# A fused graph-attention and feed-forward block in float32 on one core: the opening of the program is rewritten

## The reference, cut to what matters

```python
x = x + gnn(layernorm(x), adj, adj, Wq, Wk, Wv, bv, Wo, bo)   # x: (128, 128, 384), adj: (128, 128, 128)
x = x + ffn(layernorm(x), Wqk, bqk, Wv, bv, conv_w, conv_b, glob, pos_bias, Wg1, bg1, Wg2, bg2, Wp, bp)

def gnn(x, s, e, ...):                       # 12 heads of 32
    q, k, v = x @ Wq.T, x @ Wk.T, x @ Wv.T + bv
    scores = einsum(q, k) * 384 ** -0.5 + (s + e)
    scores = where(any(scores != 0, -1), scores, -inf)
    return (softmax(scores) @ v) @ Wo.T + bo

def ffn(x, ...):                             # 3 experts of 128, causal attention in each
    gate = softmax(relu(x @ Wg1 + bg1) @ Wg2 + bg2)      # the two largest are kept, softmax over them
    q, k = split(x @ Wqk + bqk)                          # expert 0: a 3-tap convolution over q
    y = [softmax(causal(q_e @ k_e.T * 128 ** -0.5)) @ (x @ Wv[e] + bv[e]) for e in 0, 1, 2]
    return concat(y * w_e) @ Wp + bp
```

## Time and profile before

| | before |
|---|---|
| median of three runs | 2316.46 us (2316.0 to 2317.59) |
| profiled execution, its own time | 2320.13 us |
| its span in the profile | 2318.3 us |
| PE busy | 97% |
| DVE busy | 81% |
| ACT busy | 65% |
| POOL busy | 47% |

### The profile page before, as it was taken

How to read it: one execution, slowest core, us unless ns; L and a number is a source line. 1 busy time by engine, 2 the same in 40 slices (tenths; PEclk the granted TensorE clock), 3 DMA queues, 4 the chain that set the end, 5 groups by cost and what they waited for, 6 DMA issues and landing times.

```text
span 2318.3 us, 51437 instructions
## 1 busy us (share of the span) xinstructions
PE 2238.4 (97%) x16896; PEld 1604.4 (69%) x16896; DVE 1888.0 (81%) x7395; ACT 1504.4 (65%) x5290; POOL 1101.1 (47%) x1353
## 2 busy tenths in 40 slices
PE   2799999999999999999999999999999999999998
PEld 1567777767777667777667777667777667777666
DVE  4788888888888888888888888888888888888884
ACT  2676666776666776666776666766666766666763
POOL 0454544544544544544544545544545444545442
PEclk9899999999999999999999999999999999999999
DMA  5211222211222211222211222212222112222200
GB/s 149 65 48 43 74 74 74 50 53 46 74 74 74 50 45 54 74 74 74 50 47 52 74 74 74 50 42 57 74 74 74 47 46 57 74 74 72 49 15 28
DMA packets 142265, 143.20 MB, mean 62 GB/s; under 512 B 16816, under 2 KB 141360, under 8 KB 142000
## 3 DMA queue, kind: packets, MB, share of 16 engines
q1 hardware_dynamic: 142000, 139.91, 22.7%
HBM read 39.18 MB, written 25.17 MB: 28 GB/s over the span
## 4 chain that ended last, share of the span: by engine, by line
PE 79%; DVE 16%; issue 3%; SPq 1%; ACT 0%; DMA 0%; POOL 0%; DVEq 0%; POOLq 0%
PE A_bank L468 30%; PE B_bank L468 24%; PE A_bank L528 7%; DVE raw_score L832 5%; PE B_bank L547 4%; PE A_bank L540 3%; PE A_bank L515 3%; PE B_bank L522 3%; DVE smax L839 3%; DVE V L821 3%; PE B_bank L532 2%; PE B_bank L494 2%; SPq L439 1%; DVE g_tmp L778 1%; PE A_bank L494 1%
## 5 line engine op out<-in xcount | busy, mean ns | idle before, releaser
L967 POOL TENSOR_TENSOR S<-S,rowf 128x512 f32<-128x512 f32 x384 | 389.4, 1043 | 693.5 <-DVE rowf L858 693.5
L624 ACT ACTIVATE S<-raw_score,smin 128x128 f32<-128x128 f32 x1536 | 593.2, 390 | 141.2 <-DVE smin L832 141.2
L832 DVE CUSTOM_DVE_ANT_0 raw_score<-A_bank,adj,s_unit 128x128 f32<-128x128 f32 x1536 | 444.7, 345 | 32.7 <-PE A_bank L515 32.1
L624 ACT ACTIVATION_READ_ACCUMULATOR S<-raw_score,smin 128x1 f32 x1536 | 292.3, 190 | 0.0
L638 ACT ACTIVATE PT<-A_bank 128x512 f32<-128x512 f32 x384 | 217.2, 592 | 76.9 <-PE A_bank L528 76.9
L839 DVE TENSOR_REDUCE smax<-raw_score 128x4 f32<-128x512 f32 x384 | 258.0, 679 | 0.0
L972 POOL TENSOR_TENSOR S<-S,row2f 128x384 f32<-128x384 f32 x128 | 106.0, 828 | 302.4 <-DVE row2f L866 300.6
L528 PE MATMUL A_bank<-ident,S 128*128 128x128 f32 x1536 | 217.4, 275 | 8.0 <-DVE V L821 5.3
L528 PEld LDWEIGHTS A_bank<-ident,S 128*128 128x128 f32 x1536 | 182.8, 142 | 28.5 <-DVE V L821 5.5
L642 ACT ACTIVATE yT_hi<-B_bank 128x384 fp32r<-128x384 f32 x128 | 62.3, 487 | 173.7 <-PE B_bank L547 173.6
L631 ACT ACTIVATE S<-S,s2min 128x128 f32<-128x128 f32 x384 | 149.0, 391 | 18.8 <-DVE s2min L843 18.6
(11 more groups left out here) (165 smaller groups left out, 6384.6 us busy)
## 6 DMA issues: line engine op xcount, KB each, us to landing
xin<-in_x SPq DMA_DIRECT2D x32, 768.0 KB, 4.7
Qs<-q_hi SPq DMA_DIRECT2D x256, 96.0 KB, 2.2
Ks<-k_hi SPq DMA_DIRECT2D x256, 96.0 KB, 2.7
out<-x1res SPq DMA_DIRECT2D x128, 192.0 KB, 1.9
Qs<-q_lo SPq DMA_DIRECT2D x128, 96.0 KB, 2.2
Ks<-k_lo SPq DMA_DIRECT2D x128, 96.0 KB, 2.2
adj<-in_adj SPq DMA_DIRECT2D x32, 256.0 KB, 3.5
S<-in_wq SPq DMA_DIRECT2D x1, 576.0 KB, 5.9
```

The source lines that it names most:

```text
L624: ins = nc.scalar.activation(S[b % 2][:, h, :], raw_score[c][:, j, :], ACT.Exp, bias=smin[b % 2][:, h:h + 1], scale=-1.0, accum_out=ssum[b ...
L832: ins = nc.vector.tensor_tensor_reduce(raw_score[c][:, j, :], src[:, j * T:(j + 1) * T], adj2[:, b, :], s_unit[:], 3.0e38, ALU.add, ALU.mi ...
L967: nc.gpsimd.tensor_tensor(S[b % 2][:, hs, :], S[b % 2][:, hs, :], rowf[b % 2][:, hs].unsqueeze(2).broadcast_to([P, HPC, T]), ALU.mult).the ...
```

## The change

The opening and the first two turns are rewritten; from turn 2 on the tables of order are as before.

- The maxima cross the partitions over PE: PE transposes the columns of maxima into a PSUM bank (`W.turn`), DVE reduces them to one number each (`top_col`), PE spreads these over all partitions by a matmul with the identity (`W.spread`), and DVE reads the scales from that bank. POOL's `partition_all_reduce` is gone.
- The two sets of weights are now q and k of A (`W.scale.0`) and the other four (`W.scale.1`). A semaphore `wscale_ready` lets ACT begin as soon as the scale is there, and the remaining small operations (`W.unit`) come later.
- Ten loads go to ACT's queue (five small vectors, adj, three weights in four pieces); SP issues the rest. Half of the 12 copies into `Ks` of group 0 are issued from ACT (`W.stack.1`).
- `FIRST_STEPS` gives an order of its own to turns 0 and 1. Splitting of weights (`W.hi`, `W.lo`) is spread between the other steps, `A.hT@1` and `A.qk.0@1` come ahead of the scores of group 0, and the last `qk@1` after them.
- On SP, `adj` of group 1 comes ahead of the 24 copies for group 1. Banks and counts of semaphores follow from the written order over all turns.

```diff
+FIRST_STEPS = {
+    "pe": """
+        W.turn.0@0 W.spread.0@0
+        A.hT.0@0 A.hT.1@0 A.hT.2@0 A.qk.0@0 A.qk.1@0 A.qk.2@0 A.qk.3@0 W.turn.1@0 A.qk.4@0 W.spread.1@0
...
+    "sp": """
+        A.res@0 A.stack.0@0 A.stack.1@0 A.adj@0 A.stack.0@1 A.stack.1@1
+    """,
+}
...
+def whole_program(engine):
+
+    first = [parse(word) for word in FIRST_STEPS.get(engine, "").split()]
+    order = [parse(word) for word in ORDER_OF_STEPS[engine].split()]
+    program = list(first)
+    for turn in range(2 if first else 0, NG + 2):
+        for step in order:
+            group = turn - (0 if ahead(step) else 1 if step[0] == "A" else 2)
+            if 0 <= group < NG:
+                program.append((step, group))
+    return program
...
             sp.dma_start(xin[:], dram_group(x, 0)).then_inc(x_loaded, 16)
-            sp.dma_start(adj2[:], dram_group(adj, 0)).then_inc(adj_loaded, 16)
...
-                        for j in range(HPC):
+                        for j in range(HPC // 2 if g == 0 and b == 1 else HPC):
                             sp.dma_start(heads[n * HD:(n + 1) * HD, :, j, :],
...
+                if stage == "W":
+                    n = scale_part[b].stop - scale_part[b].start
+                    if kind == "turn":
+                        pe.wait_ge(maxima, (2, 6)[b])
+                        nc.tensor.transpose(bank["B"][0][0:n, 0:P], wmax[:, scale_part[b]],
+                                            ident[:]).then_inc(maxima_turned, 1)
+                    else:
+                        pe.wait_ge(tops, b + 1)
+                        nc.tensor.matmul(bank["B"][1][:, 0:n], top_col[0:n, b:b + 1].broadcast_to([n, P]),
+                                         ident[0:n, 0:n], start=True, stop=True).then_inc(tops_spread, 1)
+                    return
...
+            act.dma_start(bqk_col[:], bqk).then_inc(consts_loaded, 16)
...
+            act.dma_start(adj2[:], dram_group(adj, 0)).then_inc(adj_loaded, 16)
+            for n in (4, 5):
+                act.dma_start(staged(raw[n][2], C), raw[n][0]).then_inc(raw_loaded[n], 16)
+            act.dma_start(staged(V2, VG)[:, :, 0:C], wv2).then_inc(raw_loaded[7], 16)
+            act.dma_start(staged(V2, VG)[:, :, C:VG], wg1).then_inc(raw_loaded[7], 16)
...
+            def weight_scales(part):
+                cols = scale_part[part]
+                n = cols.stop - cols.start
+                dve.wait_ge(maxima_turned, part + 1)
+                nc.vector.tensor_reduce(top_col[0:n, part:part + 1], bank["B"][0][0:n, 0:P], AXX,
+                                        ALU.max).then_inc(tops, 1)
+                dve.wait_ge(tops_spread, part + 1)
+                link_scale(nc.vector.tensor_scalar(wtop[:, cols], bank["B"][1][:, 0:n], TINY, None, ALU.max))
...
-            def largest(n):
-
-                pool.wait_ge(maxima, n + 1)
-                nc.gpsimd.partition_all_reduce(wtop[:, 3 * n:3 * n + 3], wmax[:, 3 * n:3 * n + 3], P,
-                                               bass.bass_isa.ReduceOp.max).then_inc(tops, 1)
```

More of the change, by code:

```diff
@@ L124, with parse, ahead @@
 }
[L128 to L136, removed]
+def parse(word):
+    word, _, group = word.partition("@")
+    stage, kind, *at = word.split(".")
+    step = (stage, kind, *([int(n) for n in at] + [0, 0])[:2])
+    return (step, int(group)) if group else step
+def ahead(step):
+    return step[0] == "A" and step[1] in ("hT", "qk", "stack")
+def whole_program(engine):
[8 more added lines that the diff above has]
+    return program
 GATE_LINKS = 17
@@ L286, in build @@
         gate_step, gate_exp = sem("gate_step"), sem("gate_exp")
[L289 to L294, removed]
+        program = {e: whole_program(e) for e in ORDER_OF_STEPS}
         def counted(step):
             return "ahead" if ahead(step) else step[0]
-        jobs = {s: [x for x in ORDER["pe"] if counted(x) == s] for s in products}
@@ L300, in build, with ordinals @@
[L300 to L306, removed]
+        def ordinals(engine, kept):
+            place, n = {}, dict.fromkeys(products, 0)
+            for step, g in program[engine]:
+                if kept(step):
+                    n[counted(step)] += 1
+                    place[step, g] = n[counted(step)]
+            return place
@@ L353, in both @@
-            def both(a, b, last):
-                for step in order:
-                    if ahead(step):
-                        if not last:
-                            do(step, following(a), False)
-                    elif step[0] == "A":
-                        do(step, a, last)
-                    elif b is not None:
-                        do(step, b, last)
-            for step in order:
-                if ahead(step):
-                    do(step, 0, False)
-            both(0, None, False)
@@ L367, in groups @@
-            both(1, 0, False)
-            for a in range(2, NG - 1):
-                both(a, a - 1, False)
-            both(NG - 1, NG - 2, True)
-            for step in order:
-                if step[0] == "B":
-                    do(step, NG - 1, True)
+            for step, g in program[name]:
+                do(step, g, g == NG - 1)
         def dram_group(t, g):
-            if isinstance(g, int):
-                return t[g * GB:(g + 1) * GB].rearrange("b t c -> t b c")
-            i, off = g
```

245 lines of the change are left out of this document (132 added, 113 removed).

## The result

The changed kernel takes 2308.49 us (median of five, 2307.82 to 2309.91). The kernel before, run beside it on the same chip, takes 2317.59 us (2316.0 to 2320.72). The ratio is 0.9957, 95% interval 0.9946 to 0.9969: 9.1 us faster, where 18.5 were forecast (2316.46 less 2298), and outside the range of 2290 to 2306. Its profiled execution took 2309.91 us, with a span of 2308.1.

What follows compares the result with a forecast made beforehand. PE was taken to bound the kernel from turn 2 on, so only turn 2's start moves: 18.1 gained, 2.3 given back, lead 16.1 at DVE's scores, 18.7 at turn 2 (117.39 to 98.7). Median 2316.46 becomes 2298, range 2290 to 2306.

Steps and rivals of the forecast that it cites:

- the waits around the all-reduce: Opening: without POOL's two "issue" waits, 11.63 and 7.56 us, PE's first product starts at 17.1 instead of 35.20, gaining 18.1.
- DVE's scores of group 0: Turn 1: 25.6 us of DVE steps plus 6.4 waiting for ACT's high parts, so the last score ends at 79.7.
- ACT then starts its first split at 13.65: Opening: maxima end at 11.6, DVE's h at 12.45, scales take 1.2; ACT splits at 13.65 instead of 25.91.
- the rival with 4.6 us: Opening: ACT's own ten load issues end at 18.24, delaying everything 4.6, to 2302.4; chance 0.22 together with PE's clock.
- PE's wait for `W.spread.1`: Before k of group 0 is complete: PE waits for DVE's maxima, v's split for second scales; 2.3 us given back.
- the copies were hidden as forecast: K's copies of group 0 land at 39.9, or 43.8 undivided, before PE reaches the scores at 44.9; splitting earns nothing.
- By the same working PE ends proj.3 at about 97: End of turn 1: the rest of group 0 (splits, norm.3, turn, mix, proj) runs beside the copies, ending about 97.
- the copies end last, by 2 us: Group 1's copies with adj take 19.0 us after DVE's last score, so they start turn 2 at 98.7.
- The rival on the clock: PE at half rate between 48 and 80 costs 6 us on group 1's products and proj: 2304; chance 0.22 with ACT's hold.
- The signs of being wrong: Rest after turn 2 changes, PE waits over 2 us between 17 and 39, or turn 2 doesn't wait for the last copy.
- From there the remaining span should be the same, to within 1 us: From PE's first score of group 1 to the end: 2318.3 less 117.4, 2200.9 us, as before.
- The rival with the banks of B: From turn 2 on: shifted loads and bank assignment cost 0.8 us or more per turn, making the kernel slower; chance 0.03.

Runs made afterwards that it cites:

- experiment 1: Changed kernel with ACT's last load, the fourth piece of weights (wg1), moved to the end of SP's list; 2305.6 us, ratio 0.9948.
- experiment 5: Changed kernel with all 24 copies of group 0 issued from SP again, K's undivided; 2308.76 us, ratio 0.9956.
- experiment 10: Experiment 1's kernel with norm.3 before ln2.0, lo.7 before proj.3, 48 unread PE transposes, and adj behind q's twelve copies; 2301.14 us, ratio 0.993.
- experiment 2: Kernel before with only the all-reduce replaced by maxima crossing over PE; order, loads and copies as before; 2306.66 us, ratio 0.9955.
- experiments 9 and 12: Both on experiment 1's kernel. 9: norm.3 first, lo.7 earlier, 48 unread PE transposes, 2305.72 us. 12: only adj behind q's copies, 2306.05 us.
- experiment 11: Changed kernel with all loads back on SP in the order of before, the 12 copies on ACT kept; 2307.12 us, ratio 0.9952.
- experiment 8: Experiment 1's kernel with 48 unread transposes behind turn.2 and mix.2 of group 0 to keep PE busy; 2305.7 us, ratio 0.9943.

## Why the prediction was wrong, step by step

The direction and the mechanism of the first gain, the waits around the all-reduce, were right. The size was wrong by half, and in the trace the loss can be added up. Forecast were 18.7 us at PE's first score of group 1; the spans differ by 10.2 (2318.3 less 2308.1).

| step of the prediction | forecast | measured | lost |
|---|---|---|---|
| first product of PE | 17.1 | 19.88 | 2.8 |
| from there until k is complete | 16.7 | 17.4 | 0.7 |
| from there until DVE's first score | 13.9 | 13.9 | 0 |
| DVE's scores of group 0 | 32.0 | 33.2 | 1.2 |
| from the last one until turn 2 | 19.0 | 18.8 | -0.2 |
| DVE behind PE in turn 2 (lead at B.hT 12.87, not 14.14) | 0 | 1.3 | 1.3 |
| the rest as long as before | 2200.9 | 2204.9, of it 1.3 in the row above | 2.7 |

**"ACT then starts its first split at 13.65" failed.** The scales were better than I took them: x wasn't late (1.1 in the sum), and they stand at 12.47, 1.2 sooner. But ACT was held until 16.42, 3.95 after them. This was the rival with 4.6 us, which shared a chance of 0.22 with PE's clock. It was decided by experiment 1. The Trainium skill, "Perfetto Trace Analysis", section "Per-instruction lifecycle", has the two issuing engines share the block that generates descriptors (its heading names DVE and SP, a note below it SP and ACT, as here). By that rule ACT's last issue was to end about where SP's did, at 18.24; it ended at 16.31, so the trace agrees roughly with the size. But the shared block as the prediction used it, the two queues in turn, isn't the reason: SP's last load is issued by 6.67, and the 8.91 us begin at 7.40. In experiment 1 two queues are busy just the same, and no load's issue takes longer than 1.65 us. What does hold the issue stays open.

**PE's wait for `W.spread.1` was near the forecast, and the copies were hidden as forecast.** k took 17.4 where 16.7 were given. From there K's last copy landed after 8.4 us, not 6.1 (45.7 less 37.3), which cost nothing. `h` of group 1 ended at 44.56, DVE's first score came 13.9 after k, and an undivided set of copies was hidden (experiment 5). The scores took 33.2 instead of 32.0, with ACT's exponentials and DVE in turns in the chain. I haven't taken these two small sizes apart.

**"By the same working PE ends proj.3 at about 97", and "the copies end last, by 2 us", failed.** I had 17.3 us from the last score to the end of `proj.3`; it took 19.0, and in the first profile of before 15.2. PE idles 4.3 us after `turn.2` and then 2.5 more, behind splits of weights that the new order has put on ACT and DVE there. It then works at the lower clock, which costs 1.4 us in `proj.2` (3.22 less 1.82) and 1.3 in `turn.3` (2.76 in the timeline, 1.47 in experiment 10). No run moved the splits. The rival on the clock had put 6 us on the products of group 1. There the clock was low as well,

```profile
61.00:75.00 14.00, 10.05 (x72) 6.80 (x73) 10.45 (x51) 10.05 (x43) 4.22 (x5) 0.76 0.00 1
```

but the chain in that stretch is made of DVE's scores and ACT's exponentials, and PE has time in hand. The price falls where PE is waited for. The copies took 18.4 us from the last score to the last landing (84.41 to 102.8) where I had 19.0, and so it is `proj.3` that ends last, by 0.6. The interval until turn 2, 18.8 for 19.0, was right by luck: it was the length of another chain than the one I had added up.

**What DVE still had to do was left out.** With `proj.3` ending so late, x, `ln2.3` and `lo.7` stand on DVE between it and the first score of group 1: 2.7 us, from 103.45 to 106.14. PE then waits for DVE twice in turn 2, and 1.3 us of the lead are gone at B.hT.

**The signs of being wrong.** The prediction named three, and all three are there. The rest of the span changed (next paragraph). PE idled about 2.3 us between its first product and the end of k (busy for 15.13 of 17.50 us from 19.80 on), beside the 2.8 us by which it began late. And the last copy wasn't what turn 2 waited for.

**"From there the remaining span should be the same, to within 1 us" failed, and this was an error of base.** One profile was taken for the kernel. In a second one the way to turn 2 is 2.7 us shorter (1.1 of it in the two "issue" gaps, 11.34 and 6.74 against 11.63 and 7.56) and the rest 4.0 longer. Against that one the changed kernel's lead at turn 2 is 11.4, not 14.1, and the span's is 11.5. The forecast subtracted a landmark worked out from durations (98.7) from one (117.39) that holds 2.7 us which the second profile doesn't have. For the way to turn 2 it isn't known which of the two is the usual one; for the rest it is the second. The rival with the banks of B, which was to add to each turn, is refuted: from the fourth on, loads of x are on average 69.73 us apart in the first profile of before, 69.79 in the second, and 69.76 and 69.75 in those of the changed kernel, where the rival needed 0.8 more in each turn to make the kernel slower.

**Profile and median.** The spans differ by 11.5 against the second profile of before, the medians by 9.1 to 9.6. A profiled execution stands for its kernel to within 1.2 us below and 2.8 above the median in these runs; before's lie at 2.5 and 2.8, the changed kernel's at 1.4 above and 0.5 below. Whether that is chance is open.

**Where the expected gain of the new order went.** Removing the all-reduce alone is worth 11.1 us (experiment 2, 2317.72 less 2306.66), and the forecast had 7 more for the whole. ACT's own loads take 3.9 of it away again. The order brings DVE's last score nearer to PE's first product: 64.2 us in experiment 1 (80.16 less 15.92), 65.6 in experiment 2 (85.72 less 20.17). From that score to B.hT, though, the new order takes 26.6 where the old one takes 23.7 (experiment 2; 23.6 and 23.0 in the kernel before). It gains 1.3 and loses 2.9. Two things lengthen that stretch. Weights are still to be split in it, which in the old order was done long before. And adj holds the copies: q's for group 1 begin 63.6 us after PE's first product in the old order, and 65.1 in the changed kernel. Neither alone is the reason, as experiments 9 and 12 show. With adj behind q's copies they begin 58.6 after the first product (experiment 10), and together with the shorter end of turn 1 the stretch takes 23.3, as in the old order; the median is 4.5 below that of experiment 1.

## What to carry to other kernels

Two chains that end together have to be shortened together: a single edit to either measures as nothing, which doesn't say that it is worth nothing. In this kernel the wait for the clock and `norm.3` hid behind the copies and the copies behind them; a two by two table of the edits (none, either, both) shows it where single experiments mislead. A load moved to an engine that computes must be priced by that engine's own queue: the last of ten loads held ACT for 8.91 us, and cost 0.74 on SP's, which has nothing to compute. Splits of weights that were spread over later steps stand in the chain again at the end of turn 1, in a stretch that grew by 2.9 us. And where a forecast is a few us of a long run, take a second profile of the kernel before: between two executions of the same program the way to turn 2 differed by 2.7 us and the rest by 4.0, in opposite directions.

## What the runs showed of the hardware

- One issue can hold an engine for 8.91 us (the fourth piece of weights on ACT's queue, behind nine others). The same load takes 0.74 from SP at 6.58 (experiment 1) and 1.76 at 16.29, behind all others (experiment 11). In the three other profiles with this load as ACT's tenth it took 8.40 to 8.83. SP issued nothing in that time, so it isn't a turn of SP's that ACT waits for; whether what is outstanding on the one queue sets it, these runs don't tell.
- Twelve copies of 96 KB were issued in 5.3 us over both queues in the changed kernel and in 8.6 on one in experiment 5. Most issues took 0.6 to 0.7 either way, and one near 38 us took 1.4 to 1.5 on each queue in use. The landings gain less: the last copy landed 8.4 us after the first issue over two queues and 10.2 over one, since a copy took 3.1 to 3.7 from issue to landing (medians) over two and 2.2 over one.
- With 4.3 us and 2.5 us without work in it, PE's granted clock was 0.57 over 12 us, a mixture of its levels of 1.2 and 2.4 GHz, and matmuls of 384 columns took 0.52 instead of 0.34. With idle transposes in the gaps it was 1.00 in the same place (experiment 8). Behind a single wait of 2.46 us it was 0.54 over 3 us (experiment 9).
- Two columns of maxima cross the partitions over PE and DVE in 2.2 us, scales included; the all-reduce on POOL took 11.34 to 11.63 us of "issue" before it and 6.74 to 7.56 after it, for an instruction that shows 0.38.

Both gaps are gone where the all-reduce is (experiment 2: POOL's two blocks of h take 1.31 us together, from 9.68). And they belong to the first call. The second one in the kernel before starts 0.14 us after the last maximum (which ends at 55.26), and DVE goes on 0.56 after that maximum:

```profile
55.40 0.39 POOL L921 PARTITION_ALL_REDUCE wtop<-wmax  x1 [22.30 <-DVE wmax L679]
55.82 0.17 DVE L690 TENSOR_SCALAR wtop<-wtop 128x3 f32<-128x3 f32 x1 [0.56 <-POOL wtop L921]
```

So in this kernel the edit removed a cost that is paid once. Whether an earlier first call would have hidden it was not tried, and whether the second has a gap behind it can't be seen, since POOL has to wait for DVE there. The Trainium skill, "GPSIMD Engine Reference", section "Instruction dispatch", puts approximately 6 us on loading a kernel's code ahead of its first call, and says that no instruction of the profile shows it. The trace agrees that the first call alone pays it and that no instruction shows it; each of the two gaps is longer than that figure, and one lies behind the call, ahead of an ordinary multiplication.
